# A cross-attention stage: row sums of the softmax weights on VectorE, weights divided on GpSimd, one more step between exponentials and transposes

## The reference

```python
x = x + _L0_xattn_ref(_layernorm(x, axis=-1), ctx_1024, L0_xattn_Wq, L0_xattn_bq, ...)
```

## Time and profile before

| what | us |
|---|---|
| median of 3 runs | 1625.49 |
| lowest and highest | 1622.92, 1629.41 |
| the profiled execution | 1629.31 |
| its span in the trace | 1627.5 |

### The profile page before, as it was taken

How to read it: one execution, slowest core, us unless ns; L and a number is a source line. 1 busy time by engine, 2 the same in 40 slices (tenths; PEclk the granted TensorE clock), 3 DMA queues, 4 the chain that set the end, 5 groups by cost and what they waited for, 6 DMA issues and landing times.

```text
span 1627.5 us, 39378 instructions
## 1 busy us (share of the span) xinstructions
PE 1508.8 (93%) x15207; PEld 1151.3 (71%) x15207; DVE 962.5 (59%) x2605; ACT 835.5 (51%) x1574; POOL 588.9 (36%) x583
## 2 busy tenths in 40 slices
PE   6999999997999899999988888869999999998998
PEld 5777776665777767777656666547888888885765
DVE  3344443346878756565568888755566776766223
ACT  4555455445777543333455766625556555553431
POOL 4343445424222101111066666632323444435024
PEclk9999999998999999999999999979999999999999
DMA  5021230000000099100000000000000000000323
GB/s 150 16 60 40 61 106 7 12 1 9 6 11 10 8 383 384 53 0 0 1 1 2 2 2 2 1 13 2 6 6 6 12 10 9 7 9 25 92 82 86
DMA packets 76527, 68.85 MB, mean 42 GB/s; under 512 B 19533, under 2 KB 57034, under 8 KB 76234
## 3 DMA queue, kind: packets, MB, share of 16 engines
q1 hardware_dynamic: 74314, 62.36, 11.9%
q0 software_dynamic: 2048, 4.20, 0.8%
HBM read 24.58 MB, written 41.96 MB: 41 GB/s over the span
## 4 chain that ended last, share of the span: by engine, by line
PE 66%; issue 14%; DVE 11%; POOL 4%; ACT 3%; DMA 1%; SPq 1%; POOLq 0%; DVEq 0%; ACTq 0%
PE bank L1864 7%; PE bank L1856 7%; PE bank L2384 5%; PE bank L2352 5%; PE bank L2346 4%; PE bank L2363 4%; PE bank L1479 3%; PE bank L1490 3%; PE bank L2375 3%; DVE s_peak L1367 3%; PE bank L1506 3%; DVE s_inverse L1394 2%; PE bank L853 2%; PE bank L3009 2%; PE bank L873 2%
## 5 line engine op out<-in xcount | busy, mean ns | idle before, releaser
L1289 ACT COPY s_pT<-bank 77x512 f32<-77x512 f32 (+1 forms) x256 | 133.6, 589 | 100.0 <-PE bank L1490 99.8
L2174 POOL TENSOR_TENSOR s_p<-s_p,s_inverse 128x616 f32<-128x616 f32 x64 | 78.3, 1229 | 229.8 <-DVE s_inverse L2297 229.8
L1716 ACT ACTIVATE s_hT<-bank,w_s_b 128x512 f32<-128x512 f32 x128 | 87.3, 687 | 126.3 <-PE bank L1856 125.3
L1193 POOL TENSOR_TENSOR s_p<-s_p,s_peak 128x1024 f32<-128x1024 f32 x64 | 120.1, 1897 | 61.9 <-DVE s_peak L1367 61.9
L1864 PEld LDWEIGHTS bank<-w_s_w2T,s_hT 128*128 128x128 f32 x1024 | 122.3, 192 | 26.8 <-issue 15.3
L1490 PE MATMUL bank<-ident,s_p 128*77 128x128 f32 (+1 forms) x1024 | 136.3, 282 | 2.8 <-ACT s_p L1282 2.0
L1490 PEld LDWEIGHTS bank<-ident,s_p 128*77 128x77 f32 (+1 forms) x1024 | 114.6, 146 | 28.8 <-issue 17.3
L1864 PE MATMUL bank<-w_s_w2T,s_hT 128*128 128x128 f32 x1024 | 124.4, 276 | 2.2 <-ACT s_hT L1716 2.2
L1282 ACT ACTIVATE s_p<-s_p 128x616 f32<-128x616 f32 (+1 forms) x128 | 110.3, 889 | 28.6 <-POOL s_p L1193 24.1
L1856 PE MATMUL bank<-s_ln_xnT,w_s_w1T 128*128 128x512 f32 x256 | 121.9, 604 | 0.0
L1817 DVE SCALAR_TENSOR_TENSOR s_total<-bank,s_combine,s_total 128x128 f32<-128x128 f32 x256 | 72.1, 344 | 74.6 <-PE bank L1864 73.2
(11 more groups left out here) (302 smaller groups left out, 3460.3 us busy)
## 6 DMA issues: line engine op xcount, KB each, us to landing
sorted_tokens<-s_zero SPq DMA_DIRECT2D x8, 4096.0 KB, 29.5
s_rows<-sorted_tokens SPq DMA_DIRECT2D x48, 64.0 KB, 1.9
routed_tokens<-s_routed SPq DMA_DIRECT2D x12, 256.0 KB, 2.4
x_all<-x SPq DMA_DIRECT2D x8, 256.0 KB, 3.0
w_s_gateup<-s_gateup SPq DMA_DIRECT2D x1, 2048.0 KB
out<-x_all SPq DMA_DIRECT2D x8, 256.0 KB, 2.8
w_s_k<-ctxT SPq DMA_DIRECT2D x8, 154.0 KB, 2.2
s_ctx<-ctxT SPq DMA_DIRECT2D x8, 154.0 KB, 2.4
```

Source lines behind the costliest of these rows:

```text
L1193: nc.gpsimd.tensor_tensor(part, part, peak[:, b % 2, HU * u:HU * (u + 1)].unsqueeze(2).to_broadcast([P, HU, keys]), ALU.subtract).then_inc ...
L1289: nc.scalar.copy(pT[0:keys, b % 2, 4 * q:4 * q + 4, :].rearrange("m h t -> m (h t)"), bank[0:keys, flip_bank("p", b, q), :]).then_inc(drai ...
L1716: nc.scalar.activation(hT[:, e % 2, c, :], bank[:, HIDDEN + k % 4, :], ACT.Gelu, bias=w.s3_b1[:, k:k + 1]).then_inc(hT_ready, 1)
```

## The change

Only the second stage's work changes (`cross`); for the fourth the same code gives the same steps with `LAG` = 1 and `DEPTH` = 2.

- The 16 products with ones in `weigh` go, with the ones. In their place DVE sums the exponentials of each head from SBUF (`inverse_of(step - 1)`, two reductions of 128x616 and a reciprocal of 128x16), between `soften(step)` and `head_outputs`.
- GpSimd multiplies the weights with that inverse, in place, in two halves (`divide`), before PE transposes them; `flip_p` waits for this (`scaled`) in place of the exponentials.
- `head_outputs` only copies the head outputs from PSUM to `oT`.
- Transposes, weighing, output and addition move by one step (`LAG` = 2), the v projection too; `p` has three buffers, and the loops run one step longer (36 in place of 35 on PE and DVE). `head_outputs` now belongs to `step - 3`, `add_to_x` and `output_of` to `step - 4`.
- The context has two buffers, and its load waits for the k projection of the group before.

The core of the diff:

```diff
@@ -1071,6 +1071,7 @@
     cross = ctxT_dram is not None
+    LAG, DEPTH = (2, 3) if cross else (1, 2)
     keys = M if cross else T
...
-    source = folded(w.s1_wk, 0, GM) if cross else xnT
+    sources = folded(w.s1_wk, 0, 2 * GM).rearrange("p (b c) -> p b c", b=2) if cross else None
...
+    scaled = sem(s + "_scaled")
+    weights_ready = scaled if cross else exp_ready
...
@@ -1139,17 +1143,17 @@
-    for step in range(BATCH + 1):
+    for step in range(BATCH + LAG):
         g = step // G + 1
         if step % G == 3 and g < GROUPS:
             take("k", g)
         for part in range(2):
-            if step:
-                take("p", step - 1, 2 * part)
-                take("p", step - 1, 2 * part + 1)
+            if step >= LAG:
+                take("p", step - LAG, 2 * part)
+                take("p", step - LAG, 2 * part + 1)
             if part == 0 and step % G == 3 and g < GROUPS:
                 take("q", g)
-            if part == 0 and step % G == 1 and step < BATCH:
+            if part == 0 and step % G == LAG and step < BATCH:
                 take("v", step // G)
...
@@ -1159,9 +1163,12 @@
     def load_ctx(sp, g):
         if g:
-            sp.wait_ge(filled, place["v", g - 1] + 1)
-        sp.dma_start(source[:, :], ctxT_dram[:, g * GM:(g + 1) * GM]).then_inc(ctx_landed, 16)
-
...
+        def divide(b):
+            for u in range(2):
+                pool.wait_ge(inverse_ready, b + 1)
+                part = p[:, b % DEPTH, HU * u:HU * (u + 1), :]
+                nc.gpsimd.tensor_tensor(
+                    part, part, inverse[:, HU * u:HU * (u + 1)].unsqueeze(2).to_broadcast([P, HU, keys]),
+                    ALU.mult).then_inc(scaled, 1)
...
         before.memory(pool)
-        nc.gpsimd.memset(ones[:, :], 0.0).then_inc(cleared, 1)
         nc.gpsimd.memset(v[:, :, :, :], 0.0).then_inc(cleared, 1)
-        pool.wait_ge(cleared, 2)
-        nc.gpsimd.memset(ones[:, :].rearrange("p (j c) -> p j c", c=STEP)[:, :, 0:DH], 1.0).then_inc(ones_ready, 1)
-        if cross:
+        if not cross:
+            nc.gpsimd.memset(ones[:, :], 0.0).then_inc(cleared, 1)
+            pool.wait_ge(cleared, 2)
+            nc.gpsimd.memset(ones[:, :].rearrange("p (j c) -> p j c", c=STEP)[:, :, 0:DH], 1.0).then_inc(ones_ready, 1)
...
@@ -1222,6 +1238,8 @@
                 own_of(b + 1)
             if not cross:
                 lower(b)
+            elif b:
+                divide(b - 1)
             g = b // G + 1
...
         if following:
             following.by_gpsimd(pool, "norm")
+        if cross:
+            divide(BATCH - 1)
+        if following:
...
@@ -1310,21 +1331,22 @@
-        for step in range(BATCH + 1):
+        for step in range(BATCH + LAG):
             b, g = step - 1, step // G + 1
-            if b >= 0:
+            if 0 <= b < BATCH:
                 exp_of(b, 0)
             if step % G == 3 and g < GROUPS:
                 keep_k(g)
-            if b >= 0:
+            if 0 <= b < BATCH:
                 exp_of(b, 1)
-                keep_pT(b, 0)
+            if step >= LAG:
+                keep_pT(step - LAG, 0)
             if step % G == 3 and g < GROUPS:
                 keep_q(g)
-            if step % G == 1 and step < BATCH:
+            if step % G == LAG and step < BATCH:
                 keep_v(step // G)
-            if b >= 0:
-                keep_pT(b, 1)
+            if step >= LAG:
+                keep_pT(step - LAG, 1)
...
@@ -1391,12 +1413,27 @@
         def head_outputs(b):
             dve.wait_ge(weighed, b + 1)
+            if cross:
+                if b >= 2:
+                    dve.wait_ge(out_done, b - 1)
+                nc.vector.tensor_copy(oT[:, b % 2, :], bank[:, WORK, A:A + T]).then_inc(o_ready, 1)
+                return
             nc.vector.reciprocal(inverse[:, :], bank[:, WORK, B:B + T]).then_inc(inverse_ready, 1)
             dve.wait_ge(inverse_ready, b + 1)
             if b >= 2:
                 dve.wait_ge(out_done, b - 1)
             nc.vector.tensor_tensor(oT[:, b % 2, :], bank[:, WORK, A:A + T], inverse[:, :],
                                     ALU.mult).then_inc(o_ready, 1)
+
+        def inverse_of(b):
+            for u in range(2):
+                dve.wait_ge(exp_ready, 2 * b + u + 1)
+                nc.vector.tensor_reduce(total[:, HU * u:HU * (u + 1)], p[:, b % DEPTH, HU * u:HU * (u + 1), :], AX.X,
+                                        ALU.add).then_inc(total_ready, 1)
+            dve.wait_ge(total_ready, 2 * b + 2)
+            if b:
+                dve.wait_ge(scaled, 2 * b)
+            nc.vector.reciprocal(inverse[:, :], total[:, :]).then_inc(inverse_ready, 1)
 
         def add_to_x(b):
...
-        for step in range(BATCH + 3):
+        for step in range(BATCH + LAG + 2):
             g = step // G + 1
-            if step >= 3:
-                add_to_x(step - 3)
+            if step >= LAG + 2:
+                add_to_x(step - LAG - 2)
             if step < BATCH:
                 soften(step)
-            if 2 <= step < BATCH + 2:
-                head_outputs(step - 2)
+            if cross and 1 <= step <= BATCH:
+                inverse_of(step - 1)
+            if LAG + 1 <= step < BATCH + LAG + 1:
+                head_outputs(step - LAG - 1)
             if step % G == 0 and g < GROUPS:
                 moments_of(g)
-            if following and BATCH - 2 <= step < BATCH + 2:
-                following.by_vector(dve, step - BATCH + 3)
+            if following and BATCH + LAG - 3 <= step < BATCH + LAG + 1:
+                following.by_vector(dve, step - BATCH - LAG + 4)
 
...
         def flip_p(b, part):
-            pe.wait_ge(exp_ready, 2 * b + part + 1)
+            pe.wait_ge(weights_ready, 2 * b + part + 1)
             for q in (2 * part, 2 * part + 1):
                 into = fill("p", b, q)
                 for j in range(4):
                     last = nc.tensor.transpose(bank[0:keys, into, j * T:(j + 1) * T],
-                                               p[:, b % 2, 4 * q + j, :], core.ident[:, :])
+                                               p[:, b % DEPTH, 4 * q + j, :], core.ident[:, :])
                 last.then_inc(filled, 1)
 
...
         def weigh(b):
 
             pe.wait_ge(drained, max(place["p", b, 3], place["v", b // G]) + 1)
-            pe.wait_ge(ones_ready, 1)
+            if not cross:
+                pe.wait_ge(ones_ready, 1)
             if b:
                 pe.wait_ge(x_ready, b)
             else:
                 before.work_bank(pe)
-            for at_column, of_lane in ((A, lambda r, j: v[0:keys, b % G, r, LANE * j:LANE * (j + 1)]),
-                                       (B, lambda r, j: ones[0:keys, LANE * j:LANE * (j + 1)])):
+            products = [(A, lambda r, j: v[0:keys, b % G, r, LANE * j:LANE * (j + 1)])]
+            if not cross:
+                products.append((B, lambda r, j: ones[0:keys, LANE * j:LANE * (j + 1)]))
...
```

More of the change, by code:

```diff
@@ L1096, in narrow_attention @@
     own = folded(w.s1_wq, 0, 2 * LANES * keys).rearrange("p (b j m) -> p b j m", b=2, j=LANES)
-    source = folded(w.s1_wk, 0, GM) if cross else xnT
-    p = peak = pT = v = ones = inverse = oT = None
+    sources = folded(w.s1_wk, 0, 2 * GM).rearrange("p (b c) -> p b c", b=2) if cross else None
+    p = peak = pT = v = ones = total = inverse = oT = None
     sem = core.plain_semaphore
@@ L1453, in project_k @@
                 pe.wait_ge(drained, place["xn", g] + 1)
-            nc.tensor.matmul(bank[:, into, 0:G * keys], t["k"][:, :], source[:, :], start=True,
+            nc.tensor.matmul(bank[:, into, 0:G * keys], t["k"][:, :], source_of(g), start=True,
                              stop=True).then_inc(filled, 1)
@@ L1466, in project_v @@
                 last = nc.tensor.matmul(bank[0:keys, into, n * D:(n + 1) * D],
[L1467 removed]
+                                        source_of(g)[:, n * keys:(n + 1) * keys], t["v"][:, :], start=True, stop=True)
             last.then_inc(filled, 1)
@@ L1530, in by_tensor @@
             return
-        for step in range(BATCH + 3):
+        for step in range(BATCH + LAG + 2):
             g = step // G + 1
-            if step >= 3:
-                output_of(step - 3)
+            if step >= LAG + 2:
+                output_of(step - LAG - 2)
             if step < BATCH:
@@ L1555, in main @@
     def main(following=None):
-        nonlocal p, peak, pT, v, ones, inverse, oT
+        nonlocal p, peak, pT, v, ones, total, inverse, oT
         with ExitStack() as local:
@@ L1564, in main @@
             v = late("_v", [P, G, LANES, LANES * STEP])
-            ones = late("_ones", [P, LANES * STEP])
-            inverse = late("_inverse", [P, T])
+            if cross:
+                total = late("_total", [P, H])
+                inverse = late("_inverse", [P, H])
+            else:
+                ones = late("_ones", [P, LANES * STEP])
+                inverse = late("_inverse", [P, T])
             oT = late("_oT", [P, 2, T])
```

46 lines of the change are left out of this document (26 added, 20 removed).

## The result

| | before | after |
|---|---|---|
| median of the runs, us | 1627.44 (1622.92 to 1629.41, 4 runs) | 1644.89 (1644.27 to 1645.60, 4 runs) |
| profiled execution, us | 1629.31 | 1644.57 |
| its span, us | 1627.5 | 1642.8 |
| DVE busy in the span, us | 962.5 | 984.9 |
| PE busy in the span, us | 1508.8 | 1498.3 |

The change makes the kernel slower: the ratio of the times is 1.0115, with a 95% interval of 1.0097 to 1.0133, 17.5 us between the medians. (Later groups of runs put the median of before between 1626.5 and 1627.6.) The spans differ by 15.3 us. From the second stage's first peak to the third stage's first copy on DVE it is 217.70 us, 15.9 more than before (201.84). The third stage takes 256.49 (256.31 before), the fourth 281.40 (281.48), the fifth 357.00 (357.01): the loss is made in the changed stage and nowhere else.

What follows compares the result with a forecast made beforehand. DVE's loop set two second-stage rounds of four, PE the others; afterwards DVE would set all. 10.7 (rounds) - 1 (head) + 2 (tail) + 1 (clock) = +12.7, about +13 on the median 1625.49: 1638.5 us, range 1630 to 1650.

Steps and rivals of the forecast that it cites:

- Rival A: Second stage: the loop through DVE sets all rounds, +9 to +18 us, 1634 to 1643; chance 0.62.
- D: Second stage: rounds at the low bound of 6.05 us, +4 to +8, given as 1631 to 1633; chance 0.18.
- What bounds the kernel: Second stage: of four rounds, two are set by DVE's loop (5.45 us), two by PE (5.98 and 6.32).
- The new round: Second stage: sums, reciprocal and copy on DVE ahead of s_oT make every round a DVE round of 6.17 us.
- 28 rounds: Second stage, batch 3 to batch 31: 162.1 us becomes 172.8, +10.7.
- What lies beside other work: Second stage: GpSimd's divisions (3.84 us of 6.17 a round, with its other work) and ScalarE's 4.2 us stay hidden.
- The port: DVE's steady rounds lose nothing beside GpSimd's divisions; only the third stage's first scaling (L149) may wait, at most one division.
- The head: Second stage's first batches: batch 2 no longer waits for the flips; -1 us, between -3 and +1.
- The tail: Second stage, batch 31's peaks to its last addition: one step more; +2 us, 0 to +4.
- The clock: Second stage: PE's idle time brings four stretches at the 1.2 GHz level, up to 0.3 us each; +1 us.
- Rival C: Second stage: the clock falls again and again, one round in three gaining 1.1 us; +23 us, 1648; chance 0.14.

Runs made afterwards that it cites:

- before_no_ones: Kernel before the change, with the second stage's 16 products with ones per batch left out (wrong values): 1620.64 us, ratio 0.9956.
- sums_behind_copy: Changed kernel with DVE's sums and reciprocal placed behind the copy of the head outputs instead of ahead of it: 1632.17 us, ratio 1.0022.
- the last experiment: Changed kernel with the last batch's two GpSimd divisions cut to one head of eight each (that batch's result wrong): 1643.76 us, measured once.
- after_keep_ones: Changed kernel with the 16 products with ones per batch put back on PE, their result unused: 1644.54 us, ratio 1.0106.
- behind_copy_spread: Kernel with the sums behind the copy, plus the next group's four moment statistics spread over a group's four steps: 1621.27 us, ratio 0.9971.
- behind_copy_keep_ones: Kernel with the sums behind the copy, plus the 16 unused products with ones per batch back on PE: 1641.47 us, ratio 1.0109.

## Why the prediction was right, and where its terms were off

The forecast was +13 us, 1638.5, within 1630 to 1650; it came out at 1644.9, +17.5 by the medians and +15.3 by the two profiles. Rival A held with its place and its reason. In size it held as a difference (+9 to +18), but the time lies 1.9 us above its 1634 to 1643: the median of before had been put at 1625.5, and with one more run it was 1627.4. The round itself came nearer to D's 6.05 than to the 6.17 of the sum. (D's +4 to +8 are 1629.5 to 1633.5, not 1631 to 1633, so its low edge lay outside the range.) The terms, forecast 10.7 - 1 + 2 + 1 = 12.7, were off in both directions: the loop +8.4, the clock inside the rounds +2.5, the head +0.8 and the tail +4.1, together 15.8 of the stage's 15.9. That the total came near is in part luck.

- **What bounds the kernel.** Right. Two rounds of four were DVE's loop, two PE's, and before_no_ones showed it to 0.01 us in 27 of 28 rounds.
- **The new round.** Forecast 6.17, measured 6.09. Of the 0.08, 0.05 is the copy: 0.23 us instead of 0.28, since the one row that I took it from (L657) was a copy at the kernel's start. The rest is in the sums (1.52 for 0.71 + 0.82) and the copy's start (0.17 for 0.18). The reciprocal, estimated at 0.25 from 8 and 128 columns, took 0.253.
- **28 rounds.** Forecast +10.7, measured 173.08 - 162.08 = +11.0, but two errors cancel. 28 x 6.09 is 170.5, +8.4. The other 2.5 us are two rounds of 7.26 and 7.43 at half clock, which belong to the clock's term.
- **What lies beside other work.** Right. GpSimd is busy 3.05 to 4.58 us a round; PE's products waited for a division once, 1.49 us at the head; in the middle of the stage only the weight loads of the flips did, three times by 0.2 us. ScalarE's 4.2 us a round stayed hidden.
- **The port.** Right as to place, too low in size: steady sums keep to 781 to 784 ns beside the divisions, and L149 alone lost 1.56 to 1.66 us (2.77 against 1.21 in the experiment and 1.11 before). That is more than the "at most one division" (1.22 us) of the prediction, because the four scalings met two divisions in a row. In after it lay off the path; in sums_behind_copy it did not. The Trainium skill's rule ("SBUF — State Buffer", section "SBUF: two separate sides") fits both: no wait for the sums, whose one SBUF input leaves GpSimd alone, and a wait for L149.
- **The head.** This term had the wrong sign. Forecast -1; measured +1.1 from batch 1's peaks to batch 3's (12.36 us, 11.25 before), and +0.8 from batch 0's (22.37 and 21.60). Batch 2 did start early, in a round of 4.52 us (5.72 before), but the next took 7.84 (5.53 before). What the term left out is a wait for the first division:

```profile
382.81 1.99 PE L1529 MATMUL bank<-ident,s_p 128*77 128x128 f32 x8 [1.49 <-POOL s_p L1208]
```

  The first flips and v, which now stand ahead of batch 3's scores, took 1.99, 1.91 and 1.68 us. That is not dearer than before, where they stood ahead of batch 2's scores and took 1.99, 1.91 and 1.56. But the half clock now reaches further: the clock of the 6.4 us ahead of batch 3 is 0.63; before it was back at 1.00 in the same place. PE had been busy 2.82 of the 16 us ahead of it, 5.99 of 14.9 before. How much of the 1.1 us is the wait and how much the clock no run separates.
- **The tail.** Forecast +2 (0 to +4), measured 19.60 - 15.51 = +4.1. The mean clock there is 0.83, before 1.00, and one set of flips took 3.70 us instead of 2.05. The port's wait was excluded by the last experiment. That the half clock makes up the miss is not shown: the tail of sums_behind_copy, at 0.91, is 19.37 us, hardly shorter (there the port's wait is on the path), and that of after_keep_ones, at 0.92, is 21.04. How the 4.1 us divide stays open.
- **The clock.** Forecast +1, four stretches at up to 0.3 us each. The number was right: four half-clock stretches begin in the 28 rounds. They cost 2.5 us there. The step that failed is the price of one: 0.14 to 0.3 us, from one round of the fourth stage. After shows that the price is not one number. Two stretches of 3.4 us cost nothing and two of 6.8 us cost 1.17 and 1.34. In the one from 452.5 to 455.9 the clock came back in time for the output product and the round stayed at 6.09; that from 401.3 on lasted 6.8 us, covered weighing, flips, output product and scores, and its round took 7.26:

```profile
401.22 0.26 DVE L1443 TENSOR_TENSOR x_all<-bank,x_all 128x128 f32<-128x128 f32 x1
...
401.63 1.93 PE L1548 MATMUL bank<-s_pT,s_v 77*32 77x128 f32 x32 [0.29 <-DVE x_all L1443]
...
403.49 3.70 PE L1529 MATMUL bank<-ident,s_p 128*77 128x128 f32 x16
...
406.98 0.64 PE L1558 MATMUL bank<-w_s_o,s_oT 128*128 128x128 f32 x2
407.54 1.04 PE L1518 MATMUL bank<-w_s_q,w_s_oT 32*128 32x308 f32 x8
```

Rival C, at 0.14, was wrong for this kernel, where it priced nine such rounds and two came, but near in its price for one (up to 1.2 us forecast, 1.17 and 1.34 measured). With the sums behind the copy it cost 9.5 us. It had deserved to be carried as a price with a spread rather than as a term of 1 us.

## What to carry to other kernels

Read a stage as one loop: which engine's chain of starts fills the whole round, and which instruction in its queue the next engine waits for. Work that nobody waits for soon belongs behind that instruction. Here exchanging two calls was worth 12.7 us of 17.5, and the same sums in front of the copy had cost their whole duration 28 times. When a change makes PE wait again and again (1.9 us once in each group here), look at the granted clock round by round, and try to spread whatever makes one step of the loop longer than the others: here that was worth another 10.9 us.

## What the runs showed of the hardware that I had not expected

- **The length of a wait alone does not tell whether the clock falls.** Ahead of the round behind the moments PE waits 1.94 us in sums_behind_copy, and the clock falls in all six groups. With the ones it waits 1.57 us, and the clock falls in none; in behind_copy_spread it waits 1.36 us, and it falls in three of six. In after PE waits 1.88 us once in each group, and a stretch follows in four of the seven groups.
- **The half clock can lock to a loop.** In sums_behind_copy it came back every group (at 403.2, 427.1, 447.5, 471.4, 495.3 and 519.2 us, four of the five distances 23.9 us), each time at the same wait of PE, and from the third on it made 5.2 into 7.2 to 7.3 us.
- **Work that nobody reads can be almost free where PE waits.** 28 us of it in after_keep_ones left the median unchanged (1644.54 and 1644.89) and made the stage 0.4 us longer; in that profile the clock stays at 1.00 over 172 us. It was not free in behind_copy_keep_ones, whose rounds PE sets.
- **Stages that nobody touched differ by 2 to 3 us** from kernel to kernel: the fourth took 278.95 us in after_keep_ones and 281.47 in sums_behind_copy. The stretch at half clock that ends it lasts 10.2 us in the one and 13.7 in the other; that this is the cause was not tested. A change in one stage is best read from that stage's own bounds.
- **Instructions in a row on DVE start before the last one ends.** Two sums of 0.782 us hold it for 1.48, two peaks for 1.50 or 1.51, and a third sum that nobody waits for added 0.70 to a round, 0.08 less than it lasts.
